# Packed levels in slot attention's first pass, four banks in its second, and expert rows gathered six tiles ahead

## What is computed

```
# slot attention, for each of 16 heads, q, k, v, w of 128 columns; w scaled to unit length, bw = beta * w
Sk = Sk * gt[None, :] + k_t[:, None] * bw[None, :]      # keys' state, decay gt = sigmoid per slot
Sv = Sv * gt[:, None] + bw[:, None] * v_t[None, :]      # values' state
a_t = softmax(q_t @ Sk * 128 ** -0.5)                   # over 128 slots
o_t = a_t @ Sv                                          # then rms norm, gate, output projection
# experts: two of 8 per token
out = sum over the two experts e of gate_e * (silu(x @ w1[e]) * (x @ w3[e])) @ w2[e]
```

## Time and profile before

| | |
|---|---|
| median of three runs | 2966.43 us |
| profiled execution, its own time | 2967.25 us |
| span in its profile | 2965.4 us |
| PE busy | 2226.3 us, 75% |
| DVE, ACT, POOL busy | 1663.5, 1107.3, 888.7 us |
| mean granted clock of PE | 0.845 |

### The profile page before, as it was taken

The page is one execution under the profiler, slowest core; times in us unless marked ns, Lnnn a source line. Parts: engine busy times, 40 slices in busy tenths (PEclk is TensorE's granted clock), DMA queues, the critical chain, the costliest instruction groups (busy, mean ns, idle before and its releaser), DMA issues. The chain is left out here.

```text
span 2965.4 us, 33448 instructions
## 1 busy us (share of the span) xinstructions
PE 2226.3 (75%) x12378; PEld 1729.2 (58%) x12378; DVE 1663.5 (56%) x1815; ACT 1107.3 (37%) x1668; POOL 888.7 (30%) x603
## 2 busy tenths in 40 slices
PE   0788888988889898889882476615734999878786
PEld 0476676666667666776671366613612666577775
DVE  7377667687676776767765500066955766320001
ACT  2445455455455454554532111122922544311110
POOL 3335454344553454544452111120010000001110
PEclk9889888888888898888986587857966999978887
DMA  1000000000000000000000244410001000055554
GB/s 55 33 17 11 10 19 17 19 18 11 10 17 19 18 11 10 18 17 18 2 3 14 87 161 163 173 48 18 1 14 41 11 18 8 3 213 204 204 209 165
DMA packets 38528, 156.65 MB, mean 53 GB/s; under 512 B 6752, under 2 KB 17376, under 8 KB 31728
## 3 DMA queue, kind: packets, MB, share of 16 engines
q1 hardware_dynamic: 33968, 142.50, 13.4%
q0 software_dynamic: 4416, 12.06, 1.2%
HBM read 145.30 MB, written 9.24 MB: 52 GB/s over the span
## 5 line engine op out<-in xcount | busy, mean ns | idle before, releaser
L764 POOL TENSOR_TENSOR sm<-score,pre 128x512 f32<-128x512 f32 x128 | 198.3, 1554 | 536.2 <-ACT score L719 414.3
L1331 DVE TENSOR_TENSOR hid_moe<-silu_moe,ps 128x384 f32<-128x384 f32 (+1 forms) x69 | 44.4, 644 | 509.6 <-PE ps L1122 509.6
L578 PE MATMUL ps<-sm,writes 128*128 128x64 f32 (+1 forms) x1920 | 285.7, 324 | 34.6 <-DVE aw L883 34.6
L578 PEld LDWEIGHTS ps<-sm,writes 128*128 128x128 f32 x1920 | 281.3, 238 | 46.6 <-issue 46.6
L779 DVE SCALAR_TENSOR_TENSOR y<-raw,small,y 128x1024 f32<-128x1024 f32 x192 | 288.8, 1505 | 34.5 <-ACT y L639 30.0
L423 PE MATMUL ps<-hT,wt 128*128 128x512 f32 x512 | 239.4, 611 | 29.3 <-ACT y L639 22.7
L1122 PEld LDWEIGHTS ps<-xt_moe,w_moe 128*128 128x128 f32 x2024 | 248.3, 202 | 7.3 <-ACT xt_moe L1177 3.2
L829 DVE TENSOR_TENSOR pairs<-kq,const 128x512 f32<-128x512 f32 x112 | 168.2, 1502 | 147.2 <-ACT kq L688 147.2
L1122 PE MATMUL ps<-xt_moe,w_moe 128*128 128x128 f32 x2024 | 247.1, 284 | 1.9 <-ACT xt_moe L1177 1.9
L509 PE MATMUL ps<-pairs,wt_t 128*128 128x64 f32 x1792 | 231.2, 286 | 17.8 <-DVE score L844 16.0
L509 PEld LDWEIGHTS ps<-pairs,wt_t 128*128 128x128 f32 x1792 | 225.4, 204 | 22.8 <-issue 22.8
(11 more groups left out here) (294 smaller groups left out, 4125.2 us busy)
## 6 DMA issues: line engine op xcount, KB each, us to landing
w_moe<-in_moe SPq DMA_DIRECT2D x23, 1792.0 KB, 7.6
w_moe<-in_moe SPq DMA_DIRECT2D x23, 1024.0 KB, 5.2
w_moe<-in_moe SPq DMA_DIRECT2D x23, 896.0 KB, 10.1
w_moe<-in_moe SPq DMA_DIRECT2D x23, 512.0 KB, 6.3
wt<-in_gsa SPq DMA_DIRECT2D x16, 640.0 KB, 3.9
beta<-beta_all SPq DMA_DIRECT2D x16, 512.0 KB, 3.4
fT_c<-in_fT SPq DMA_DIRECT2D x4, 1024.0 KB, 4.9
planes_moe<-y_rows SPq DMA_DIRECT2D x8, 512.0 KB, 5.7
```

The lines of the kernel that those rows point to most:

```text
L578: last = mm(ps[:, l % 2, i * w:(i + 1) * w], writes[:, l * N + tile * P:l * N + (tile + 1) * P], sm[:, (l % 2) * HN + i * w:(l % 2) * HN + ...
L764: g.tensor_tensor(packed(sm[:, (l % 2) * HN:(l % 2 + 1) * HN], l), halves(score[:, :], l)[1], packed(pre[:, l * HN:(l + 1) * HN], l), ALU. ...
```

## The change

In the first pass every level is packed: POOL writes the left halves densely into `dense` (three buffers of 128x512), PE turns 4 tiles in place of 8, and `read` is 4 matmuls of 128 columns at each level. The products of k and q are made afresh at each level (`cross`, 4 matmuls), from the packed left halves of k (ACT's new `pack_k`) and the right halves of q; DVE's `near` masks and scales them straight from PSUM, and `kq` and its two copies are gone. ACT's new `spread` copies `dense` into the left halves of `writes` for the second pass. In the second pass the products use banks 0, 1, 4 and 5, so that `products(l)` waits for the merge of level l - 4. In `moe` the gathers run 6 tiles ahead and the scatters have 4 buffers. The masks in `const` grow by 320 columns.

```
-                for n in range(NT):
-                    mm(ps[:, n // 4, (n % 4) * P:(n % 4 + 1) * P], Y(p, "k")[:, n * P:(n + 1) * P],
-                       Y(p, "q")[:, n * P:(n + 1) * P], start=True, stop=True)
...
+                def cross(l):
+                    n = LEVELS * h + l
+                    if l >= 2:
+                        pe.wait_ge(s("kq_pairs"), n - 1)
+                    if 0 < l < LEVELS - 1:
+                        pe.wait_ge(s("k_left"), (LEVELS - 2) * h + l)
+                    for b in range(B):
...
+                        last = mm(ps[:, 2 + l % 2, b * P:(b + 1) * P], left.rearrange("p n h -> p (n h)") if l in (0, LEVELS - 1) else left,
+                                  halves(Y(p, "q")[:, b * T:(b + 1) * T], l)[1], start=True, stop=True)
+                    last.then_inc(s("kq_ps"), 1)
+                cross(0)
                 if before:
                     pe.wait_ge(s("own"), h)
                 pe.wait_ge(s("qk"), h + 1)
                 ones_sum(4, front_sum).then_inc(s("qk_ps"), 1)
+                cross(1)
...
-                    for i, tile in enumerate(range(NT) if l < LEVELS - 1 else range(0, NT, 2)):
-                        c = l * N + tile * P
-                        last = nc.tensor.transpose(ps[:, 2 * (l % 2) + i // 4, (i % 4) * P:(i % 4 + 1) * P], writes[:, c:c + P], ident)
+                    for b in range(B):
+                        last = nc.tensor.transpose(ps[:, l % 2, b * P:(b + 1) * P],
+                                                   dense[:, (l % 3) * HN + b * P:(l % 3) * HN + (b + 1) * P], ident)
...
-                        for i in range(NT):
-                            c = (l % 2) * HN + i * (P // 2)
-                            last = mm(ps[:, 4 + l % 2, i * (P // 2):(i + 1) * (P // 2)], wt_l[:, i * P:(i + 1) * P],
-                                      pairs[:, c:c + P // 2], start=True, stop=True)
...
+                    for b in range(B):
+                        c = slice((l % 2) * HN + b * P, (l % 2) * HN + (b + 1) * P)
+                        last = mm(ps[:, 4 + l % 2, b * P:(b + 1) * P], wt_t[:, c], pairs[:, c], start=True, stop=True)
...
                     if l >= 1:
                         read(l - 1)
+                        if l + 1 < LEVELS:
+                            cross(l + 1)
...
                     pe.wait_ge(s("reads"), n + 1)
-                    if l >= 2:
-                        pe.wait_ge(s("aw_level"), n - 1)
+                    if l >= 4:
+                        pe.wait_ge(s("aw_level"), n - 3)
+                    elif l >= 2:
+                        pe.wait_ge(s("own"), h + 1)
+                    pe.wait_ge(s("spread"), n + 1)
...
-                act.wait_ge(s("kq_ps"), h + 1)
-                A(kq[:, 0:N], pair(0), ACT.Copy, scale=SCALE)
-                A(kq[:, N:], ps[:, 2, :], ACT.Copy, scale=SCALE).then_inc(s("kq"), 1)
+                pack_k(h, p, 1)
...
-                        A(wt_t[:, (l % 2) * N:(l % 2) * N + w], pair(l % 2)[:, 0:w], ACT.Copy).then_inc(s("writes_t"), 1)
+                        A(wt_t[:, (l % 2) * HN:(l % 2 + 1) * HN], ps[:, l % 2, :], ACT.Copy).then_inc(s("writes_t"), 1)
+                        if l + 2 < LEVELS - 1:
+                            pack_k(h, p, l + 2)
+                        spread(h, l)
...
-                    g.tensor_tensor(halves(writes[:, l * N:(l + 1) * N], l)[0], halves(Y(p, "w"), l)[0], sl,
+                    if l >= 3:
+                        pool.wait_ge(s("writes_t_ps"), LEVELS * h + l - 2)
+                        pool.wait_ge(s("spread"), LEVELS * h + l - 2)
+                    g.tensor_tensor(packed(dense[:, (l % 3) * HN:(l % 3 + 1) * HN], l), halves(Y(p, "w"), l)[0], sl,
                                     ALU.mult).then_inc(s("writes"), 1)
...
+                def near(l):
+                    dve.wait_ge(s("kq_ps"), LEVELS * h + l + 1)
+                    own, products = pairs[:, (l % 2) * HN:(l % 2 + 1) * HN], ps[:, 2 + l % 2, :]
...
+                    return v.tensor_tensor(by_b(own), by_b(products), m, ALU.mult)
...
-            for j in range(3):
+            for j in range(AHEAD):
                 gather(j)
             pool.wait_ge(s("dst_row"), 1)
             for j in range(TILES):
                 scatter(j)
-                if j + 3 < TILES:
-                    gather(j + 3)
+                if j + AHEAD < TILES:
+                    gather(j + AHEAD)
```

More of the change, by code:

```diff
@@ L132, in shared @@
         signals=[],
-        gathered=[ctx.enter_context(nc.semaphore(f"gathered{i}")) for i in range(3)],
-        scattered=[ctx.enter_context(nc.semaphore(f"scattered{i}")) for i in range(2)],
+        gathered=[ctx.enter_context(nc.semaphore(f"gathered{i}")) for i in range(AHEAD)],
+        scattered=[ctx.enter_context(nc.semaphore(f"scattered{i}")) for i in range(BEHIND)],
     )
@@ L1038, in _ @@
                 sp.dma_start(w[:, c + UP:c + W], own[:, UP:W]).then_inc(s(f"down_weights{j % 3}"), 16)
-            for slot in range(2):
-                sp.wait_ge(scattered[slot], scattered_by(TILES - 2 + (TILES + slot) % 2))
+            for j in range(TILES - BEHIND, TILES):
+                sp.wait_ge(scattered[j % BEHIND], scattered_by(j))
             for half in range(2):
```

97 lines of the change are left out of this document (49 added, 48 removed).

## The result

The changed kernel takes 2679.68 us (median of 4 runs, 2674.69 to 2689.85), the kernel before in the same session 2968.05 us (4 runs). The ratio is 0.9037, with a 95% interval of 0.9002 to 0.9071: faster by 9.6%. The prediction said 2720 us, range 2650 to 2800. The profiled execution took 2682.16 us, 37.6 us less than the sum of the prediction.

A forecast was written before the change was run, and what follows sets the result against it. No single engine bounds the kernel: experts wait for gathered rows, slot attention's limit moves between engines. 2967.25 - 98.0 - 93.4 (experts) - 46.5 (second pass) - 9.6 (first pass) = 2719.8, so 2720 us; range 2650 to 2800 us.

The forecast's parts named there:

- The gathers: Expert stages: PE's wait for gathered rows ends, tiles take 6.0 and 9.9 us, saving 98.0 + 93.4 = 191.4 us.
- the bound by 296 GB/s: Expert stages: at the highest slice's rate a tile's bytes need 6.2 us (first stage) and 10.2 us (second).
- The prediction's other version: Expert stages: at 358 GB/s from HBM, PE stays the limit at 5.62 and 9.78 us a tile; sum 2710 us.
- The second rival: Expert stages: weights become the limit, tiles take 7.8 and 11.5 us, 68 us more, 2788 us; 12%.
- The second pass: Slot attention's second pass: four banks end DVE's waits for PE's products, 3.1 us in 15 heads, 46.5 us saved.
- The first pass: Slot attention's first pass: output projection start unmoved, from there to first projection 0.6 us less a head, 9.6 us saved.
- The rival of the slow clock: First pass: PE, with gaps in each level, falls to clock 0.50, 32 us more a head, some 3230 us; 2%.
- The signs to look for: Head 86 us (wrong over 89, under 82), tiles 6.0 and 9.9 (wrong over 7, 11), DVE's waits gone, POOL's `pre` waits longer.

The follow-up runs named there:

- weights5: Changed kernel with five weight buffers in place of three in the first expert stage alone; 2670.47 us, ratio 0.9019 to the kernel before.
- banks_only: Kernel before with only the four banks for the second pass's products and the waits that go with them; 2917.6 us, ratio 0.9840.
- cross_twice: Changed kernel with each first-pass level's products of k and q made twice on TensorE; 2687.97 us, ratio 0.9062 to the kernel before.
- early_pre: Changed kernel with ACT's level 1 prefix copy moved ahead of its copy of level 0's turned writes; 2655.66 us, ratio 0.8972 to the kernel before.
- early_chain: Changed kernel, ACT's prefix copies for levels 0 and 1 ahead of the copy of o, level 2's ahead of the first turned writes; 2630.7 us, ratio 0.8882.
- shift32: Changed kernel with 32 more idle instructions (long-met waits) ahead of PE's loop over the heads; 2647.35 us, ratio 0.8944 to the kernel before.
- packed_only: Changed kernel with the second pass and row buffers of before, so the packed first pass stands alone; 2920.18 us, ratio 0.9868 to the kernel before.
- gathers_only: Kernel before with only the gathers six tiles ahead and the scatter's buffers four deep; 2761.18 us, ratio 0.9312.

## Why the prediction was right, and where it was not

- **The gathers** (191.4 us). Right: three more tiles of room took PE's wait for rows from 127.5 us to nothing. Of the two sizes, the first stage's tile is 6.15 us (6.0), 3 us less gained over the 20 tiles; the second's is 9.49 us (9.9), 8 us more. The wrong term is the bound by 296 GB/s, a slice that held idle time: it made me take 9.9 between 9.78 and 10.2, and the second stage ran below its own 9.78 us, which I had read from a tile whose `up` took 6.52 us where the later ones take 6.25. In the first stage not the rate was short, but the time between the issue of a load and its use (weights5). The prediction's other version, by the 358 GB/s of the Trainium skill (DMA: Bandwidth & Descriptors, Where 436 GB/s comes from), had PE stay the limit: that is what the second stage shows, and the first once its loads come early. No stretch of some length that I read shows that rate; the highest is 333 GB/s over 90 us. Single slices of 1.8 us go above it, up to 400 GB/s (changed kernel, 1627 to 1700 us).
- **The second rival** (weights become the limit, 2788 us) was the right place with a much too high price: 0.5 us a tile in one stage.
- **The second pass** (46.5 us). Right in each step and in size: banks_only measured 46.6 us, from own products to `collect` 3.15 us went, PE rests ahead of `collect`, and `collect` kept its slow clock (5.17 us).
- **The first pass** (9.6 us). This step failed. I took the start of the output projection as unmoved, since ACT had more to do, and from there to the first projection counted 0.6 us of PE's work. Measured were 1.62 and 1.70 us. I had summed up work per engine and left out the waits between them. In the second of the two pieces, at full clock, 0.99 us is PE's wait for DVE's addition to xT, which is gone. The masked products in DVE's queue just there took 1.54 to 1.75 us each and now take 0.68 us; I had counted that saving for DVE and put none of it on the path. That this is why the wait went is argued from the two timelines, not tested. To the output projection the pass is a chain across POOL, ACT, PE and DVE. In the heads behind no branch it fell from 25.0 to 22.4 us, more than the table's 1.62, which also contains the heads that the stall slowed. cross_twice put 7.1 us of work on PE, of which 2.7 to 3.4 us reached the time, so PE is a part of the chain and not the whole; early_pre and early_chain took 19 and 46 us off by moving copies alone, with no work less. I had seen POOL wait 0.80 us for `pre`, called ACT's queue full, and not looked at the head's beginning. There the trace of before already shows two longer waits for the same copy, with ACT idle behind another step:

```profile
859.05 1.04 POOL L759 TENSOR_TENSOR prefix<-prefix 128x512 f32<-128x512 f32 x1 [4.55 <-ACT pre L661]
...
865.41 1.04 POOL L759 TENSOR_TENSOR prefix<-prefix 128x512 f32<-128x512 f32 x1 [2.37 <-ACT pre L661]
```

How the 3.3 us divide over these steps wasn't taken apart.
- **What wasn't forecast at all**: the stall at the branch, which came with the packed pass's program and hangs on where its loop lies. Without it (shift32) the changed kernel is at 0.8944, 28 us faster by the ratios; (84.7 - 82.6) x 15 = 31.5 us by the copies of o.
- **The balance.** The profiled execution is 37.6 us under the sum. Second stage -8.2, first stage +2.9; from the first to the last copy of o the heads gave 73.8 us in place of 55.5: -18.3; and head 0 ended at 209.0 in place of 222.2, where 0.6 was expected: -12.6. Together -36.2. Of head 0's part some 7 to 10 us go with the packed pass (it ends at 211.9 in packed_only, at 218.6 in banks_only and 219.6 in gathers_only); what in it does this I didn't follow up. So a third of the miss has no known cause, and that the rest is as small as it is owes something to luck: the stall took back half of what the first pass gave beyond its 0.6 us.
- **The rival of the slow clock** didn't come. From 400 to 1400 us the granted clock rose from 0.89 to 0.94. But the first pass didn't keep its full clock throughout: besides `collect`, the lower clock is seen at the output projection behind a wait of 2.4 us for DVE, in 8 of 14 heads (10 before), and behind the stall at the branch.
- The signs to look for: a head of 84.7 us lies within 82 to 89, the tiles within 7 and 11 us, DVE's waits after the convolution are gone. POOL's wait for `pre` grew a little, from 88.3 us in 30 waits to 100.5 in 38 (from 400 to 1400 us), but its long waits are for levels 0 and 1, not 3 and 4, where I had put them.

## What to carry to other kernels

A pass in which four engines hand work on can't be priced by summing up each engine's work: double one engine's share for a test, read from the trace what of it arrives (the clock and a stall elsewhere may move with it, as in cross_twice), and where much of it doesn't, look for the engine that idles in front of a step whose input is ready, because another step stands ahead of it in its queue. A wait for a load that shows up without a releaser may be too little room between issue and use; compare the rate over the whole stage before calling it bandwidth. And when a loop's program becomes shorter or longer, look at its branch and at the instruction fetches: 32 idle instructions ahead of it were worth some 30 us here, more than half of what four banks gave.

## What the runs showed of the hardware

- PE's loop (808 matmuls and 808 weight loads a turn) was fetched anew, 51 blocks of 16 KB in 1000 us, or kept (one fetch), by where it lay; a shift of 256 instructions restored the first state. The stall was 3.2 to 4.5 us a branch, and in cross_twice, with 936 matmuls a turn, only 0.5 to 1.2 us, with 56 fetches. So fetches alone don't make the stall. What decides its size stays open.
- The first expert stage moved 333 GB/s over 90 us when loads were issued earlier (weights5), above the 296 GB/s of the highest slice in the earlier trace rows.
- The same four matmuls of the output projection took 1.98 us in some heads and up to 3.67 us in others of the changed kernel, behind the same wait of 2.4 us for DVE.
- DVE's product with beta took 2.08 us beside POOL's reads; its product of q and k, of the same size, took 1.20 us 5 us later, with POOL at rest. I didn't test the cause.
